# Sixteen-headed cross-attention: half of each unit's softmax shift by ScalarE's bias from PSUM, the other half by VectorE

## What is computed

```
qh, kh, vh = split(q @ Wq + bq), split(k @ Wk + bk), split(v @ Wv + bv)   # 16 heads of 8; layer 0: relu, no bias
E = 8 ** -0.5 * einsum('bqhd,bkhd->bhqk', qh, kh)                          # layer 1: masked keys are left out
A = softmax(E, axis=-1)
out = einsum('bhqk,bkhd->bqhd', A, vh)                                     # layers 1 and 2: @ Wo + bo
```

## Time and profile before

| | us |
|---|---|
| median of 3 runs (1831.24 to 1834.42) | 1834.31 |
| the profiled execution | 1829.58 |
| its span, first to last instruction | 1827.8 |
| TensorE busy in the span (matmuls) | 1253.5 |
| VectorE busy | 1221.3 |
| ScalarE busy | 765.0 |
| POOL busy | 155.1 |

### The profile page before, as it was taken

The page is one execution under the profiler, slowest core; times in us unless marked ns, Lnnn a source line. Parts: engine busy times, 40 slices in busy tenths (PEclk is TensorE's granted clock), DMA queues, the critical chain, the costliest instruction groups (busy, mean ns, idle before and its releaser), DMA issues.

```text
span 1827.8 us, 25228 instructions
## 1 busy us (share of the span) xinstructions
PE 1253.5 (69%) x8858; PEld 833.6 (46%) x8870; DVE 1221.3 (67%) x3005; ACT 765.0 (42%) x1410; POOL 155.1 (8%) x131
## 2 busy tenths in 40 slices
PE   5998889843599999889932488987889800001665
PEld 2555555522468888745521344554564400001444
DVE  2654557878656666577768667785773479994446
ACT  1444446633355445346534432665433413440221
POOL 2211003100000000021111000210000000000001
PEclk7888789976699999989955677999999955555678
DMA  3000300000000000000000000000001310001000
GB/s 113 13 13 13 135 7 7 8 1 0 1 1 1 1 1 6 2 12 7 7 1 0 0 1 7 7 7 1 0 0 38 75 37 0 1 0 52 12 6 23
DMA packets 28806, 28.12 MB, mean 15 GB/s; under 512 B 12192, under 2 KB 23456, under 8 KB 27808
## 3 DMA queue, kind: packets, MB, share of 16 engines
q1 hardware_dynamic: 28704, 26.76, 4.9%
HBM read 20.20 MB, written 6.55 MB: 15 GB/s over the span
## 4 chain that ended last, share of the span: by engine, by line
PE 45%; issue 23%; DVE 20%; ACT 7%; DVEq 2%; POOL 1%; DMA 1%; SPq 1%; POOLq 0%; ACTq 0%
PE PSA L993 3%; PE PSA L840 3%; PE PSA L830 3%; PE PSA L1278 2%; DVE BIG L2477 2%; PE PSA L680 2%; PE PSA L686 2%; PE PSA L663 2%; PE PSA L1010 2%; PE PSA L973 2%; ACT BIG L1480 2%; PE PSA L947 2%; PE PSA L959 2%; PE PSA L954 2%; DVE BIG L2469 1%
## 5 line engine op out<-in xcount | busy, mean ns | idle before, releaser
L1305 PE MATMUL PSA<-W,TMP 128*128 128x128 f32 x32 | 8.3, 441 | 215.5 <-DVE TMP L2499 215.5
L1487 ACT ACTIVATE QK<-PSA 128x512 f32<-128x512 f32 x192 | 104.7, 595 | 109.9 <-PE PSA L840 109.9
L526 POOL TENSOR_TENSOR RSTD<-VEPS,HALF 128x4 f32<-128x4 f32 x50 | 50.7, 1014 | 966.2 <-DVE VEPS L1798 966.2
L1917 DVE TENSOR_TENSOR BIG<-PSA,MX 128x1024 f32<-128x1024 f32 x96 | 117.6, 1225 | 10.9 <-PE PSA L840 8.0
L830 PE MATMUL PSA<-BIG 32*128 32x512 f32 x384 | 113.5, 680 | 14.8 <-DVE BIG L1917 13.7
L1913 DVE TENSOR_REDUCE MX<-PSA 128x8 f32<-128x1024 f32 x96 | 116.9, 1218 | 5.3 <-PE PSA L830 4.7
L1480 ACT ACTIVATE BIG<-BIG 128x1024 f32<-128x1024 f32 x96 | 101.7, 1060 | 25.2 <-DVE BIG L1917 25.2
L840 PE MATMUL PSA<-K,BIG 128*128 128x128 f32 x768 | 106.6, 284 | 6.4 <-ACT BIG L1480 4.8
L840 PEld LDWEIGHTS PSA<-K,BIG 128*128 128x128 f32 x768 | 90.3, 146 | 39.4 <-ACT BIG L1480 27.8
L1305 PEld LDWEIGHTS PSA<-W,TMP 128*128 128x128 f32 x32 | 7.1, 327 | 216.7 <-DVE TMP L2499 216.7
L1111 PE MATMUL PSA<-K,BIG 128*128 128x128 f32 x128 | 31.5, 412 | 107.8 <-DVE BIG L2151 107.8
(11 more groups left out here) (378 smaller groups left out, 3121.5 us busy)
## 6 DMA issues: line engine op xcount, KB each, us to landing
CTX<-in_ctx_t SPq DMA_DIRECT2D x16, 256.0 KB, 3.1
W<-in_w SPq DMA_DIRECT2D x1, 2048.0 KB, 7.4
W<-in_w SPq DMA_DIRECT2D x1, 1412.0 KB, 12.0
ROWS<-in_rows SPq DMA_DIRECT2D x1, 1232.0 KB, 8.7
scratch_q<-TMP SPq DMA_DIRECT2D x4, 256.0 KB, 2.0
W<-scratch_q SPq DMA_DIRECT2D x64, 16.0 KB
W<-in_w SPq DMA_DIRECT2D x2, 512.0 KB, 10.9
scratch_q<-BIG SPq DMA_DIRECT2D x4, 256.0 KB, 2.3
```

Source lines behind the costliest of these rows:

```text
L526: pool.tensor_tensor(RSTD[:, 0, :], VEPS[:, 0, :], HALF[:], ALU.pow).then_inc(ln_rstd.sem, 1)
L1487: act.activation(PT[:, m % 2, c, :], PS[4 + c], ACT.Copy).then_inc(p_ready.sem, 1)
L1917: dve.tensor_tensor(tile(PH[:, m % 2, :], 8), s, last(high, P), ALU.subtract).then_inc(shifted.sem, 1)
```

## The change

The row maximum is now taken negated, and its second half (four heads of the unit) is given to ScalarE as the bias of the exponential, which reads those scores from PSUM, one head at a time: four instructions of 128x128. VectorE subtracts for the first four heads only, and ScalarE takes their exponential in one instruction of 128x512, behind the four. The factor 8 ** -0.5 moves from the exponential into the keys: VectorE makes scaled copies of the key biases and lanes (KB, LANES) in seven small instructions at the start of the kernel, ScalarE waits for them before its first work, and the key activations take the factor and the scaled columns. `exp_ready` counts two events for a unit. Scores wait, besides `shifted`, for the first of the two of unit m-2; transposes, copies and product take the second bank's heads first, each half behind its own event.

```diff
-        exp_ready = signal("exp_ready", units)
+        exp_ready = signal("exp_ready", {**units, **each(CROSS3, 2 * HALVES)})
...
                     if m >= 2:
                         pe.wait_ge(shifted.sem, shifted.at(p, 0, m - 2))
+                        pe.wait_ge(exp_ready.sem, exp_ready.at(p, 0, 2 * (m - 2)))
...
                 def transposes(m):
-                    pe.wait_ge(exp_ready.sem, exp_ready.at(p, 0, m))
-                    for c in range(2):
+                    for k, c in enumerate((1, 0)):
+                        pe.wait_ge(exp_ready.sem, exp_ready.at(p, 0, 2 * m + k))
                         if m:
-                            pe.wait_ge(p_ready.sem, p_ready.at(p, 0, 2 * (m - 1) + c))
+                            pe.wait_ge(p_ready.sem, p_ready.at(p, 0, 2 * (m - 1) + k))
...
         @block.scalar
         def _(act):
             act.wait_ge(inputs_loaded, 48)
+            act.wait_ge(setup_dve, 1)
...
-                    act.activation(KN[:, new % 2, :], bank, func, bias=col(f"{p}.bk")).then_inc(k_ready.sem, 1)
+                    act.activation(KN[:, new % 2, :], bank, func, scale=float(HD) ** -0.5, bias=KB[:, CROSS3.index(p), 0:1]).then_inc(k_ready.sem, 1)
...
                 def exp(m):
+                    act.wait_ge(max_taken.sem, max_taken.at(p, 0, m))
+                    if m >= 2:
+                        act.wait_ge(t_psum.sem, t_psum.at(p, 0, 2 * (m - 2)))
+                    for j in range(4):
+                        ins = act.activation(PH[:, m % 2, tok(4 + j)], PS[2 * (m % 2) + 1][:, tok(j)], ACT.Exp,
+                                             bias=MX[:, 8 * (m % 2) + 4 + j:8 * (m % 2) + 5 + j])
+                    ins.then_inc(exp_ready.sem, 1)
                     act.wait_ge(shifted.sem, shifted.at(p, 0, m))
-                    act.activation(PH[:, m % 2, :], PH[:, m % 2, :], ACT.Exp, scale=float(HD) ** -0.5).then_inc(exp_ready.sem, 1)
+                    act.activation(PH[:, m % 2, 0:T], PH[:, m % 2, 0:T], ACT.Exp).then_inc(exp_ready.sem, 1)
...
             dve.wait_ge(inputs_loaded, 48)
+            for n, p in enumerate(CROSS3):
+                dve.tensor_scalar(KB[:, n, 0:1], col(f"{p}.bk"), float(HD) ** -0.5, None, ALU.mult)
+                at = C_AT[f"{p}.bklane"][0]
+                dve.tensor_scalar(KB[:, n, 1:5], COLS[:, at:at + 4], float(HD) ** -0.5, None, ALU.mult)
+            at = C_AT["lane"][0]
+            dve.tensor_scalar(LANES[:], COLS[:, at:at + 4], float(HD) ** -0.5, None, ALU.mult)
+            dve.drain()
...
-                    dve.tensor_reduce(high, s, AX_X, ALU.max).then_inc(max_taken.sem, 1)
+                    dve.tensor_reduce(high, s, AX_X, ALU.max, negate=True).then_inc(max_taken.sem, 1)
...
-                    dve.tensor_tensor(tile(PH[:, m % 2, :], 8), s, last(high, P), ALU.subtract).then_inc(shifted.sem, 1)
+                    dve.tensor_tensor(tile(PH[:, m % 2, 0:T]), s[:, 0:4], last(high[:, 0:4], P), ALU.add).then_inc(shifted.sem, 1)
```

More of the change, by code:

```diff
@@ L162, in decoder @@
         HALF = sb("HALF", [P, GB])
+        KB = sb("KB", [P, 3, 5])
+        LANES = sb("LANES", [P, 4])
         ONES = sb("ONES", [P, P])
@@ L848, in product @@
                         pe.wait_ge(ov_ready.sem, ov_ready.at(p, 0, n - 1))
-                    for c in range(2):
-                        pe.wait_ge(p_ready.sem, p_ready.at(p, 0, 2 * m + c))
+                    for k, c in enumerate((1, 0)):
+                        pe.wait_ge(p_ready.sem, p_ready.at(p, 0, 2 * m + k))
                         for j in range(4):
@@ L1484, in copies @@
                         act.wait_ge(pv_done.sem, pv_done.at(p, 0, m - 2))
-                    for c in range(2):
-                        act.wait_ge(t_psum.sem, t_psum.at(p, 0, 2 * m + c))
+                    for k, c in enumerate((1, 0)):
+                        act.wait_ge(t_psum.sem, t_psum.at(p, 0, 2 * m + k))
                         act.activation(PT[:, m % 2, c, :], PS[4 + c], ACT.Copy).then_inc(p_ready.sem, 1)
@@ L1500, in cross_attention @@
                 for r in range(2):
-                    ins = act.activation(KM[:, 0, :, r, :], tile(PS[4]), func, scale=col("lane", r), bias=col(f"{p}.bklane", r))
+                    ins = act.activation(KM[:, 0, :, r, :], tile(PS[4]), func, scale=LANES[:, r:r + 1], bias=KB[:, CROSS3.index(p), 1 + r:2 + r])
                 ins.then_inc(k_ready.sem, 1)
@@ L1950, in cross_attention @@
                     if p == "L0x":
-                        ins = dve.tensor_scalar(KM[:, 0, :, r, :], tile(PS[3]), 0.0, col("lane", r), ALU.max, ALU.mult)
+                        ins = dve.tensor_scalar(KM[:, 0, :, r, :], tile(PS[3]), 0.0, LANES[:, r:r + 1], ALU.max, ALU.mult)
                     else:
-                        ins = dve.tensor_scalar(KM[:, 0, :, r, :], tile(PS[3]), col(f"{p}.bk"), col("lane", r), ALU.add, ALU.mult)
+                        ins = dve.tensor_scalar(KM[:, 0, :, r, :], tile(PS[3]), col(f"{p}.bk"), LANES[:, r:r + 1], ALU.add, ALU.mult)
                 ins.then_inc(km_ready.sem, 1)
```

## The result

The changed kernel took 2008.74 us, median of four runs (1984.37 to 2033.57), beside 1833.62 for the kernel before (1831.24 to 1834.42), 175 us more. The ratio is 1.087 with a 95% interval of 1.079 to 1.095; it rests on the two runs within 1.5% of the fastest, 1984.37 and 2000.41, whose mean, 1992.39, lies 159 us above the mean before, 1833.22, while the profiled execution, 2017.06, is one of the two longer ones. Six more runs in a later experiment gave 1990.11 to 2023.26. The forecast was 1940 with a range of 1900 to 2010, so the median lies inside it by one microsecond, and the forecast itself is 69 us too low.

A forecast was written before the change was run, and what follows sets the result against it. No engine was full; waits between TensorE and ScalarE bound the three cross-attention stages. Added: 92 us for the longer loop, 12 half clock, 1.5 start, 106 in all; forecast 1940 us, 5.8% slower, range 1900 to 2010.

The forecast's parts named there:

- What bounds the loop, and the new wait: Cross-attention stages: a 2.83 us loop of transposes, copies, exponential; scores waiting for ScalarE's first exponentials enter it, making 4.03 us.
- the forecast's plain step: One unit without other work: 0.75 to first copy, 0.97 copies, 1.20 exponentials, 0.05 signal, 1.06 scores; 4.03 us.
- The four exponentials: ScalarE's added 128x128 exponentials from PSUM with a column as bias: 1.20 us a unit, range 1.14 to 1.44.
- the 452 of the sum: The three cross-attention stages after the change, at full clock: 451.6 us against 359.4 before, 92 us more.
- VectorE's saving at nothing: The halved subtraction saves VectorE 51 us over 96 units, costed at nothing because that engine was mostly waiting.
- Half clock at the start of a stage: First units of L0x, L2x and L1x (3 + 3 + 1) at half clock, 1.7 us more each: 12 us.
- TensorE loses its clock: Rival: gaps in each unit drop TensorE to half clock, about 2155 us if all; chance 0.21 for more than 1985.
- The 682 us: The three stages if all at half clock: 217 us a stage and 249 for L1x, 323 more than before.
- the 2040: The time in us given for a third of the time at half clock.
- the row held against that rival: Profile row of L1x's last units: 65% busy, gaps like those to come, clock at 1.00 for 10 us.
- VectorE as the bound: Rival: VectorE's 0.53 us a unit is all on the path and the new wait met early, 1783 us; chance 0.05.
- Other work hidden: Rival: values, projections and output copies find room beside the loop, about 1878 us; chance 0.06 for 1838 to 1905.

The follow-up runs named there:

- The wait alone: Kernel before the change, with only one wait added: scores of unit m wait for the whole exponential of unit m-2; 1975.7 us beside 1829.45, ratio 1.076.
- the run that reads SBUF: Changed kernel without the new wait: VectorE subtracts all eight heads, ScalarE takes its four small exponentials from SBUF; 1857.52 us beside 1829.45, ratio 1.015.
- the kernel with both behind: Changed kernel with scores of unit m+3 and values brought back both issued behind the product of unit m on TensorE; 1847.53 us beside 1832.9, ratio 1.009.

## Why the prediction was right, and where not

**What bounds the loop, and the new wait: right.** The step that decided the sign held as written: scores wait for exponentials that stand behind the copies on ScalarE, and transposes stand behind the scores on TensorE. The wait alone makes a kernel 7.6% slower, and taking the scores out of its way gives 134 to 150 us back.

**The sizes of the steps: right.** At full clock with masks the forecast's plain step is 4.03 + 0.54 = 4.57 us, and 4.59 was measured; with values and output copy 5.50, and 5.52 was measured. The four exponentials took 1.15, not 1.20, at the lower bound. (The Trainium skill, "ScalarE: Activation LUTs", section "What ACT_TABLE_LOAD costs", led to an estimate of 1.27; the trace is 9% below it from PSUM, and at 1.27 in the run that reads SBUF.) Against that, the signal from the small exponentials to TensorE took 0.14 and not the 0.05 of the earlier trace rows. Over 93 steps that is 8 us more, against 5 less for the exponentials. The stages at full clock, 461 us, are 7 above the 452 of the sum with the 2.4 us from first to last start of a unit's transposes in three stages; the other 4 are within what the estimate can tell.

**VectorE's saving at nothing: nearly right.** It is worth 7 us in the kernel before. In the kernel with both behind, where the loop is as before, it did not show.

**Half clock, 12 us: the mis-sized term.** The step "Half clock at the start of a stage" counted seven units at the starts of stages. By the estimate of the table 84 us of the profiled execution's stages are half clock. From 1935 to that execution's 2017.1 it is 82 us: 84 - 12 = 72 of clock, 7 of steps and 3 around the stages. At 1992.39, 25 us less, some 60 would be half clock if the difference is clock alone, as the list of times and clocks suggests; no profile of those runs was taken. The prediction named a clock under 0.9 over a whole stage as a sign that it is wrong, and it came in all three stages. The rival "TensorE loses its clock" came true together with the forecast's mechanism, as a third to two thirds of each stage at half, not as one case or the other. Its price was good, 5.7 us for a plain step and 5.73 measured; a step with values costs 7.70 where its terms give 7.1. Two figures made from that price are off. The 682 us leave out that the last two steps issue no scores, some 5 us a stage: 667, a ratio of 1.48, and by it the 84 would be 80. And the 2040 is what half of the steps at half clock would give; for a third of the time 682 and 452 give about 1985.

That the median lies in the stated range is owed to the part of it that was kept for this rival, and that it does so by one microsecond is luck: three of the ten runs lie above 2010, none in the forecast's own 1922 to 1974, and one below 1985, where the rival's chance of 0.21 begins. At the other end, 0.07 below 1900 leaves out the 0.06 given to 1838 to 1905.

The argument that failed is the row held against that rival: L1x's end, 65% busy and 10 us at 1.00. Two neighbouring windows of the changed kernel in L2x, one in L0x, and the two microseconds in the kernel before that begin 2 us behind that row show why such a row proves little:

```profile
1290.00:1300.00 10.00, 7.28 (x68) 4.22 (x67) 4.29 (x6) 6.76 (x18) 6.20 (x4) 1.00 0.00 0
1300.00:1310.00 10.00, 7.22 (x55) 4.28 (x54) 4.21 (x14) 6.06 (x16) 1.04 (x1) 0.66 0.01 3
...
418.00:430.00 12.00, 10.37 (x60) 5.95 (x60) 6.32 (x10) 5.55 (x14) 0.00 (x0) 0.50 0.01 1
...
922.00:924.00 2.00, 1.56 (x7) 1.56 (x8) 0.00 (x0) 1.98 (x10) 0.00 (x0) 0.50 0.00 0
```

In the kernel before the clock was at 0.50 from 922 on, 2 us after the row at 1.00 ends: the row stops short of a fall. In the changed kernel TensorE is busy for 73% at 1.00, for 72% in the next 10 us, in which it falls, and for 86% at 0.50 without rising. Half clock makes the work itself longer, so its busy share rises while the clock stays low. (The Trainium skill, "TensorE: Matmul & The Clock Gate", section "A second HAM failure mode: psum-queue depth-cycling", tells of a clock that goes back and forth when TensorE is idle for short times between groups of matmuls. The gaps of 0.8 to 1.9 us in every step and the clocks of 0.67 to 0.84 agree with it.) The other row, L0a at 72% busy with a mean of 0.65, was the nearer one: it repeats a pattern of bursts and gaps (0.52 to 1.60 us) as the changed stages do. It should have had a price in the sum, not only a chance.

**The other rivals.** VectorE as the bound is refuted by the 7 us. Other work hidden would give plain and even steps alike; 4.59 and 5.52 refute it.

**What stays open:** why the clock rises and falls when it does, at like busy shares and gaps; and the 9 us outside the stages of the kernel with both behind.

## What to carry to other kernels

When a consumer moves to another engine, write down the in-order queue of that engine and ask what stands ahead of the new releaser: an instruction that was beside the loop (here the scores) can enter it, and moving it in its own queue can give most of the loss back, here 134 to 150 us of 159 to 175. When a change opens a gap in every step of a loop on TensorE, price the half clock as a term of the sum, from stretches that repeat the same gaps over many steps. Taking time off an engine that runs ahead of the others buys next to nothing: 51 us of VectorE's were worth 7.

## What the runs showed of the hardware

The granted clock at nearly the same work was 1.00 in one 10 us window and fell in the next, at 73 and 72% busy. Matmuls whose result nobody reads made the kernel 31 to 47 us faster where TensorE waited anyway; more of them ahead of work took 11 and 38 us of that back. Four 128x128 exponentials with a column as bias took 1.15 us from PSUM and 1.27 from SBUF. TensorE's timeline of the changed kernel in L2x shows a fall and a rise:

```profile
1297.39 1.13 PE L833 MATMUL PSA<-BIG 32*128 32x512 f32 x4 [1.37 <-ACT BIG L1487]
...
1302.94 1.84 PE L833 MATMUL PSA<-BIG 32*128 32x512 f32 x4 [1.94 <-ACT BIG L1487]
...
1309.35 2.08 PE L833 MATMUL PSA<-BIG 32*128 32x512 f32 x4 [0.84 <-ACT BIG L1487]
...
1317.95 2.08 PE L833 MATMUL PSA<-BIG 32*128 32x512 f32 x4 [1.84 <-ACT BIG L1487]
...
1324.60 1.13 PE L833 MATMUL PSA<-BIG 32*128 32x512 f32 x4 [0.84 <-ACT BIG L1487]
```

Four scores take 1.13 us at 2.4 GHz and 2.08 at 1.2. The fall comes in the scores behind a gap of 1.94 us, and by 1324.60 they are back at 1.13, behind a gap of 0.84; at 1309.35 a gap of 0.84 had not brought it back.
